# The layout of the split expert weights in DRAM: chunks of 512 columns in place of one long row per partition

## The reference

```
x = x + ga * linear_attention(layernorm(x) * (1 + ca) + sa)      # 32 heads of 64
h = layernorm(x) * (1 + cb) + sb
# mixture of experts: 8 experts, each token uses 2
probs = softmax(h @ gate_w.T); top 2, renormalised -> rw
g, u = h @ gate_proj_w[e].T, h @ up_proj_w[e].T                  # 512 -> 256
out_e = (silu(g) * u) @ down_proj_w[e].T                         # 256 -> 512
x = x + gb * sum_e rw[e] * out_e
# second block: a token-wise tuple layer, then a gated FFN with 2:4 sparsity
x = x + ga1 * rmsnorm_layer(...);  x = x + gb1 * sparse_ffn(...)
```

## Time and profile before

| | |
|---|---|
| median of 3 runs | 2043.15 us (2042.33 to 2045.4) |
| the profiled execution's own time | 2050.34 us |
| its span | 2048.6 us |
| mean granted PE clock | 0.94 of full speed |
| PE, DVE, POOL, ACT busy | 89%, 60%, 36%, 34% |
| DMA | 220.27 MB in 83905 packets, 108 GB/s on the mean |
| queue q1 (SP) | 59872 packets, 167.37 MB |
| WB<-ws_d | 8 DMAs of 3072 KB, median 14.4 us from issue to landing |
| ws_d<-W | 18 DMAs of 1024 KB and 12 of 512 KB, median 6.4 and 6.6 us |
| u_d<-yt,sm | 39 accumulating DMAs, median 5.2 us |

### The profile page before, as it was taken

One profiled execution on the slowest core, in us unless ns is written; L12 is line 12 of the kernel. 1 busy time (PEld: TensorE's weight loads), 2 busy tenths in 40 slices (PEclk: granted clock), 3 DMA queues, 4 the chain that ended last, 5 costly groups with the idle time before them and its releaser, 6 DMA issues.

```text
span 2048.6 us, 25401 instructions
## 1 busy us (share of the span) xinstructions
PE 1825.1 (89%) x8300; PEld 1432.1 (70%) x8300; DVE 1234.1 (60%) x2172; ACT 687.6 (34%) x1321; POOL 727.4 (36%) x681
## 2 busy tenths in 40 slices
PE   8889999999999999988547877956689999999996
PEld 5557888888888888866446666635477778787784
DVE  4547666666666666686833333379856666656564
ACT  2434444545444544422112221123332222213220
POOL 1436121212121221111344443446745455536442
PEclk9999999999999999998658988988899999999998
DMA  6211454545353535420668877720200111001011
GB/s 231 83 63 59 134 155 134 154 134 154 116 150 105 167 90 173 113 72 26 202 206 260 241 200 230 150 66 21 62 26 13 44 32 47 14 22 51 6 52 42
DMA packets 83905, 220.27 MB, mean 108 GB/s; under 512 B 6396, under 2 KB 30988, under 8 KB 81264
## 3 DMA queue, kind: packets, MB, share of 16 engines
q1 hardware_dynamic: 59872, 167.37, 25.5%
q0 software_dynamic: 11616, 28.98, 6.7%
q10 hardware_dynamic: 12336, 22.89, 3.7%
HBM read 128.11 MB, written 91.11 MB: 107 GB/s over the span
## 4 chain that ended last, share of the span: by engine, by line
PE 68%; DVE 18%; DMA 6%; issue 4%; ACT 2%; POOL 1%; ACTq 0%; DVEq 0%; POOLq 0%; SPq 0%
PE bank L717 20%; PE bank L719 20%; PE bank L718 20%; DMA u_d<-yt,sm 5%; PE bank L783 2%; PE bank L908 2%; DVE hh L1959 2%; PE bank L1003 1%; DVE st L1450 1%; DVE rr L1720 1%; DVE na L1432 1%; DVE na L1431 1%; PE bank L748 1%; POOL hs_d L2142 1%; PE bank L934 1%
## 5 line engine op out<-in xcount | busy, mean ns | idle before, releaser
L1720 DVE RECIPROCAL rr<-rr 128x256 f32<-128x256 f32 x128 | 218.9, 1732 | 4.7 <-ACT num L1186 4.7
L717 PE MATMUL bank<-hT,W1b 128*128 128x512 f32 x512 | 210.3, 411 | 10.9 <-DVE hh L1914 10.9
L717 PE MATMUL bank<-W1a,hT 128*128 128x512 f32 x512 | 209.7, 410 | 3.4 <-DVE hT L1634 3.4
L718 PE MATMUL bank<-hT,W1b 128*128 128x512 f32 x512 | 205.0, 400 | 0.0
L719 PE MATMUL bank<-hT,W1b 128*128 128x512 f32 x512 | 204.7, 400 | 0.0
L719 PE MATMUL bank<-W1a,hT 128*128 128x512 f32 x512 | 202.2, 395 | 0.0
L718 PE MATMUL bank<-W1a,hT 128*128 128x512 f32 x512 | 201.1, 393 | 0.0
L2051 POOL TENSOR_TENSOR x<-x,tmp 128x512 f32<-128x512 f32 x64 | 101.2, 1582 | 261.4 <-DVE tmp L1712 261.4
L1739 DVE SCALAR_TENSOR_TENSOR kt<-bank,kt 128x256 fp32r<-128x256 f32 x128 | 50.8, 397 | 176.0 <-ACT vt L1202 175.8
L1914 DVE TENSOR_TENSOR hh<-hh,bank 128x512 f32<-128x512 f32 x64 | 43.2, 687 | 188.5 <-PE bank L719 160.5
L1979 POOL TENSOR_TENSOR W<-stage,W 128x1024 fp32r<-128x1024 f32 x32 | 76.8, 2399 | 189.6 <-ACT W L1094 187.3
(11 more groups left out here) (265 smaller groups left out, 4610.8 us busy)
## 6 DMA issues: line engine op xcount, KB each, us to landing
hs_d<-bor SPq DMA_DIRECT2D x24, 1548.0 KB, 11.5
WB<-ws_d SPq DMA_DIRECT2D x8, 3072.0 KB, 14.4
ws_d<-W SPq DMA_DIRECT2D x18, 1024.0 KB, 6.4
stage<-wa SPq DMA_DIRECT2D x32, 512.0 KB, 5.3
stage<-wbe SPq DMA_DIRECT2D x24, 512.0 KB, 4.1
stage<-wdn SPq DMA_DIRECT2D x24, 512.0 KB, 3.9
mw<-wmod SPq DMA_DIRECT2D x10, 1024.0 KB, 4.8
hg<-hs_d ACTq DMA_DIRECT2D x39, 258.0 KB, 4.8
```

What stands on the lines that cost most here:

```text
L717: pe.matmul(o, lhs(HI), rhs(HI), start=start, stop=False, **kw)
L718: pe.matmul(o, lhs(HI), rhs(LO), start=False, stop=False, **kw)
L1720: dve.reciprocal(rr[:, pair, h], rr[:, pair, h]).then_inc(r_rec, 1)
```

## The change

`ws_d` keeps its size, but its order in DRAM becomes: expert, half, chunk of 512 columns, partition, column. One chunk of one half is now a block of 128 rows of 2,048 bytes. The load of an expert then moves 12 rows of 2,048 bytes for each partition, where it moved one of 24,576. The stores change to match: those of slices 0 to 2 become two DMAs each (one for each half) with rows of 2,048 bytes, where they were one with rows of 4,096; those of slice 3 keep their form. All waits on `e_stored` count accordingly. The tile `WB` in the core's memory and all instructions of PE, DVE and POOL stay as they are.

```diff
-    ws_d = nc.dram_tensor("ws_d", (GE, P, 2, 3072), F32, kind="Internal").ap()
+    ws_d = nc.dram_tensor("ws_d", (GE, 2, 6, P, 512), F32, kind="Internal").ap()
...
             def we_store(g, j):
                 x = j % 2
                 sp.wait_ge(split_done, split_e_at(g, j) + 1)
-                if j < 3:
-                    sp.dma_start(ws_d[bass.ds(g - 1, 1), :, :, j * 1024:(j + 1) * 1024].rearrange("a p s n -> p (a s) n"),
-                                 esp[:, x, :, :].bitcast(F32)).then_inc(e_stored[x], 16)
-                    return
                 for half in (HI, LO):
-                    sp.dma_start(ws_d[GE - 2:GE, :, half, bass.ds((g - 1) * 512, 512)].rearrange("e p n -> p e n"),
-                                 esp[:, x, half, :].rearrange("p (e n) -> p e n", e=2).bitcast(F32)) \
-                        .then_inc(e_stored[x], 16)
+                    if j < 3:
+                        sp.dma_start(ws_d[bass.ds(g - 1, 1), half, 2 * j:2 * j + 2, :, :].rearrange("a c p n -> p (a c) n"),
+                                     esp[:, x, half, :].rearrange("p (c n) -> p c n", c=2).bitcast(F32)) \
+                            .then_inc(e_stored[x], 16)
+                    else:
+                        sp.dma_start(ws_d[GE - 2:GE, half, bass.ds(g - 1, 1), :, :].rearrange("e a p n -> p (e a) n"),
+                                     esp[:, x, half, :].rearrange("p (e n) -> p e n", e=2).bitcast(F32)) \
+                            .then_inc(e_stored[x], 16)
...
-                sp.dma_start(WB[:, e % 2, :, :].bitcast(F32), ws_d[e]).then_inc(w_all, 16)
+                sp.dma_start(WB[:, e % 2, :, :].bitcast(F32).rearrange("p s (c n) -> p (s c) n", n=512),
+                             ws_d[e].rearrange("s c p n -> p (s c) n")).then_inc(w_all, 16)
...
-                        act.wait_ge(e_stored[0], g * 32)
-                        act.wait_ge(e_stored[1], g * 48)
+                        act.wait_ge(e_stored[0], g * 64)
+                        act.wait_ge(e_stored[1], g * 64)
```

More of the change, by code:

```diff
@@ L554, in load_x_again @@
                 if b < 2:
-                    sp.wait_ge(e_stored[0], 32 * (GA - 2))
-                    sp.wait_ge(e_stored[1], 48 * (GA - 2))
+                    sp.wait_ge(e_stored[0], 64 * (GA - 2))
+                    sp.wait_ge(e_stored[1], 64 * (GA - 2))
                 else:
@@ L1221, in step_a @@
                 if b == 2 and not (first or last):
-                    act.wait_ge(e_stored[0], (g - 1) * 32 + 16)
+                    act.wait_ge(e_stored[0], (g - 1) * 64 + 32)
                     split_e(g, 2)
-                    act.wait_ge(e_stored[1], (g - 1) * 48 + 16)
+                    act.wait_ge(e_stored[1], (g - 1) * 64 + 32)
                     split_e(g, 3)
@@ L1480, in apply_rows @@
                 if b == 1:
-                    dve.wait_ge(e_stored[0], 32 * (GA - 2))
-                    dve.wait_ge(e_stored[1], 48 * (GA - 2))
+                    dve.wait_ge(e_stored[0], 64 * (GA - 2))
+                    dve.wait_ge(e_stored[1], 64 * (GA - 2))
                 if b >= 2:
```

## The result

The changed kernel takes 2027.39 us (median of 4 runs, 2027.11 to 2027.75), against 2044.16 (2042.33 to 2045.4) for the kernel before in the same comparison: 16.8 us faster, a ratio of 0.9919 with a 95% interval of 0.9902 to 0.9936. The forecast was 2004, with a range of 1988 to 2032. The sign is right and the time lies in the range, but the gain is less than half of the 39 us forecast, and close to rival 1 (2024).

A forecast was written before the change was run, and what follows sets the result against it. The prediction took PE in the slots stage to be bound by adds to DRAM slowed beside expert loads. Gains of 33.3 us (experts 3 to 7) and 5.7 (expert 2), 39 us off 2043.15, gave 2004 us, range 1988 to 2032.

The forecast's parts named there:

- rival 1: Adds beside a load stay at 8 us or more, as POOL's gathers and ACT's loads join in: 2024 us, chance 0.17.
- What bounds the stage, and by which path: Slots stage: PE waits for DVE's product, DVE for adds slowed by expert loads; about 59 us hang on this.
- The stores, and stage A: Stage A: 18 more store DMAs of about 0.6 us on SP are covered, with PE as the bound; cost 0.
- The load of expert 2: Slots stage, PE's two gaps behind this load: both shrink to 2.8 us, clock left low; gain 5.7 us.
- The time of an add beside the new load: Slots stage: 4.9 us alone plus 1.5 to 2.6 us beside 2,048-byte packets, taken as 7.0 us.
- The formula for a gap: Loads of experts 3 to 7: an add may take 8.1 us, two 13.0; a gap of 1.9 us is left.
- The clock: PE behind the remaining 1.9 us gaps: its clock stays high, saving 2.3 us at each of five loads.
- The load itself: Expert load in small packets: lands after 16.4 us, just fits; cost 0, at worst 1 us at two or three experts.
- rival 4: The yielding load lands late and PE waits at `w_all`; with landing after 30 us, 25 us slower, 2068; chance 0.07.
- The sum: Whole kernel: 33.3 us at experts 3 to 7 plus 5.7 at expert 2, 39 us off 2043.15, gives 2004.
- Taking packets in turn: Each DMA engine takes packets from SP, POOL and ACT one by one; a round falls from 1.12 to 0.35 us.
- The third rival: The DMA engines' turn is not one 2,048-byte packet, so nothing is won and the time stays 2043; chance 0.07.

## Why the prediction was right and wrong

**What bounds the stage, and by which path.** Right. PE waits at line 965 for DVE, DVE for an add, the add for a load. Taking the loads away won 47.5 us, the packet alone, with the layout untouched, gave the gain of the change, and eight entries in `sm` took PE's wait for the adds away.

**The stores, and stage A.** Right: 878.02 us busy in 900 against 877.79.

**The load of expert 2.** Right: 5.7 us forecast. The gaps of 7.44 and 3.87 us became 5.09 and 0.99, that is 5.2 us. The split was luck: both were to be 2.8 us. The first add took 9.3 us where 7.0 was taken, and the one beside the `mst` packets 8.5 where 9.7 was kept.

**The time of an add beside the new load.** This step failed: "I take 7.0". Measured are 8.7 to 10.7 us for the add that starts with the load, and 6.3 to 8.3 for the one behind it. The 4.9 us alone were right, and they hold the accumulation already. What was too small is the excess over it, 1.5 to 2.6 us, from two plain transfers of ACT beside x<-u_d. Measured is 4.8 us, for the add and for the plain scatter alike, and 5.5 us for ACT's own row loads and for the gathers. Beside x<-u_d only the queues of SP and ACT moved packets; beside an expert's load POOL's did too. That is the reason rival 1 gave, and it fits, but no run took POOL's or ACT's transfers away, so it is argued and not shown. That the plain scatter landed in about the 7 us forecast for the add is chance. The row with POOL's add beside small packets, 9.71 us beside 4,096 bytes, I used as the upper bound; it was the right size for the add that starts with the load, and no upper bound.

**The formula for a gap.** It holds with the right time in it: the add of 10.29 us at 1160.79 exceeds the allowed 8.1 by 2.2 us, and PE's gap at 1171.80 is this one (the adds of 9.2 us beside the loads of experts 6 and 7 exceed it by 1.1, and the gaps are 1.08 and 1.33):

```profile
1171.80 0.33 PE L967 MATMUL bank<-ident,pps 128*128 128x128 f32 x1 [2.17 <-DVE pps L1834]
```

In the loads of experts 3 to 7, the gaps at line 965 before were 32.0 us and are 17.6 now (23.7 less 5.09 and 0.99). So 14.4 us are won where 31.3 - 9.5 = 21.8 were forecast: 7.4 short.

**The clock.** "I take it as high" failed for the longer gaps: 11.5 us forecast, 5.1 measured. In this stage products ran at the lower clock behind gaps of 1.70, 2.17, 2.42, 3.98 and 5.09 us and at the higher one behind those of 0.99, 1.04, 1.33, 1.36 and 1.41, though the gap of 1.69 in stage D had left it high. The one near row was right at its place and wrong at the next. Nor does the length alone decide: in the kernel before with 8 entries a gap of 2.46 us left the clock high.

**The load itself.** Forecast to land by 16.4 us and just to fit. It took 16.2 to 19.2 and was late three times, 2.4 us in all. The price named was "at worst 1 us at each of two or three", which is nearly this. The cover was counted wrong in one place: rival 4 gives the load of expert 7 one slot more than 14.6 us, but it was issued at 1239.93 and PE waited for it at 1256.3, so its cover was 16 us, that of four slots and a gap. Rival 4's mechanism is real, small here, and it sets the bound once the adds have room.

**The sum.** In the profiled executions: 39 less 7.4 (gaps), 6.4 (clock), 2.4 (late loads) and 0.5 (expert 2) is 22.3; the spans differ by 22.7. The last 6 us to the 16.8 of the medians are the profiled execution of before, which stood 6 us above its median. I subtracted all of a gain worked out on it from the median.

**Taking packets in turn.** Half right. In the stretch from 1162 to 1170 after, with a load under way (columns as in the earlier trace rows):

```profile
q1 hardware_dynamic: 632, 1.29, 48.2%
q0 software_dynamic: 238, 0.58, 33.6%
q10 hardware_dynamic: 244, 0.45, 16.2%
```

SP's queue moves 632 packets against 238 and 244. So the counts no longer run together as they did with 24,576 bytes (114, 162, 165). In like stretches SP moved 183 packets to POOL's 146 with 12,288 bytes, 434 to 219 with 4,096 and 972 to 208 with 1,024. A packet of POOL still takes 0.18 us (33.6% of 16 x 8 us over 238), but an engine moves one only every 0.54 us (16 x 8 us over 238) where the round was to take 0.35. Either an engine takes several of SP's small packets in a turn, or POOL's and ACT's queues do not have a packet ready in each; the counts do not tell which.

The third rival was the rule in the Trainium skill (DMA: Bandwidth & Descriptors, section on queues, rings and completion order) that a turn is a run of 9 to 17 descriptors. In this kernel that is the load's twelve rows of 2,048 bytes as one turn, and the time would have stayed at 2043. For the step from 24,576 to 2,048 bytes the runs speak against it, with 13.7 to 14.8 us going to 8.7 to 10.7. Between 4,096 and 2,048 bytes the add's time hardly changes, and there these runs cannot tell how many packets make a turn. The row pitch rule of the Trainium skill (the same page, section on latency and other measured facts) is for the pitch from one partition to the next, and puts 207 GB/s at 512 KiB beside 214 at the full rate. Here the 256 KiB lie between the packets of one partition, and they cost nothing that shows: the time was that of the old layout with the same packet size.

## What to carry to other kernels

When small transfers that others wait for run beside a large one, look at the size of the large one's packets: in DMAs of 2,048 to 4,096 bytes a row the small ones took 9 to 11 us in place of 14 to 15, and the layout in DRAM did not have to change for that, only the split of the load. With 1,024 bytes they took 7 to 8, but the load itself came late. Before taking an excess from the nearest row, ask what else was moving beside that row: beside two busy queues the excess was 1.5 to 2.6 us, beside three it was 4.8. Before calling an operation the cause, look at what it costs alone. And check whether a deeper buffer takes the latency off the path: eight small entries won 21 us by themselves.

## What the runs showed of the hardware

- An indirect DMA that accumulates takes 4.9 us alone. Where it starts with a load whose packets are of 24,576, 12,288, 4,096, 2,048 and 1,024 bytes it takes 13.7 to 14.8, 12.0 to 12.9, some 10, 8.7 to 10.7 and 7.2 to 8.4 us. The same scatter without accumulation takes 2.8 alone and 6.8 to 8.2 beside 2,048 bytes: 2 us less in both places.
- SP took longer to issue DMAs behind a load in small packets: eight of them took 11.94 us behind 2,048-byte packets, 8.36 behind 4,096 and 4.22 behind 24,576. Nothing waited for them here.

```profile
1094.61 11.94 SPq L671 DMA_DIRECT2D mst<-winout  x8
```

- The load of expert 0, with little beside it, took 13.3 us in packets of 2,048 bytes, and 11.5 in packets of 24,576. That of expert 1, beside POOL's scatters of the routing, took 18.6 against 11.8.
